# Attention heads: strict turns between VectorE and GpSimd, a 672/352 split, and one row maximum a step over 1024 columns

## The reference, cut to what matters

```python
qn = _scramble(qn); kn = _scramble(kn)                       # 64 rows a head
helical = jnp.einsum('bhpsc,bhptc->bhst', qn, kn) / p
dot = jnp.einsum('bshd,bthd->bhst', qh, kh) / math.sqrt(hd)
attn = jax.nn.softmax(0.5 * dot + 0.5 * helical, axis=-1)
out = jnp.einsum('bhst,bthd->bshd', attn, vh).reshape(b, s, e)
return out @ Wo.T + bo
```

## Time and profile before

| what | us |
|---|---|
| median of 3 runs (5178.03 to 5193.08) | 5188.1 |
| the profiled execution's own time | 5184.21 |
| its span, first to last instruction | 5182.4 |
| first `probs` to last `high` of the attention heads | 2652.7 to 4842.8 |
| VectorE busy over the span | 4091.0 (79%) |
| TensorE busy (matmuls) over the span | 3695.5 (71%) |
| ScalarE busy | 3058.9 (59%) |
| GpSimd busy | 2570.1 (50%) |

### The profile page before, as it was taken

The page is one execution under the profiler, slowest core; times in us unless marked ns, Lnnn a source line. Parts: engine busy times, 40 slices in busy tenths (PEclk is TensorE's granted clock), DMA queues, the critical chain, the costliest instruction groups (busy, mean ns, idle before and its releaser), DMA issues. The chain is left out here.

```text
span 5182.4 us, 68093 instructions
## 1 busy us (share of the span) xinstructions
PE 3695.5 (71%) x15374; PEld 1420.1 (27%) x15374; DVE 4091.0 (79%) x7784; ACT 3058.9 (59%) x4256; POOL 2570.1 (50%) x2075
## 2 busy tenths in 40 slices
PE   7984002222322697897679999999999999999568
PEld 3431001211212242343223333333333333333123
DVE  5535969999998455358789999999999999998352
ACT  5566212222221454245649898989989898999342
POOL 1000757777777101204626666666666666666312
PEclk9997556666666898999979999999999999999779
DMA  1015653333432200012431111111111111100300
GB/s 45 6 45 118 114 117 75 86 79 75 91 75 56 72 13 10 0 72 102 163 62 36 36 35 36 36 29 27 36 36 36 36 35 36 36 21 5 106 10 33
DMA packets 126542, 276.41 MB, mean 53 GB/s; under 512 B 41296, under 2 KB 70864, under 8 KB 117904
## 3 DMA queue, kind: packets, MB, share of 16 engines
q1 hardware_dynamic: 124208, 263.05, 21.4%
q10 hardware_dynamic: 1952, 9.18, 0.6%
HBM read 178.65 MB, written 93.36 MB: 52 GB/s over the span
## 5 line engine op out<-in xcount | busy, mean ns | idle before, releaser
L1027 POOL TENSOR_TENSOR att_heads_rest<-att_heads_probs,att_heads_high 128x576 f16<-128x576 f32 x1024 | 1393.1, 1361 | 830.9 <-ACT att_heads_high L1114 824.3
L1144 DVE TENSOR_REDUCE att_heads_maxima<-att_heads_peek 128x1 f32<-128x512 f32 x2048 | 1311.2, 680 | 94.2 <-PE att_heads_peek L1040 66.6
L1112 ACT ACTIVATE att_heads_probs<-att_heads_scores 128x1024 f32<-128x1024 f32 x1024 | 1073.4, 1048 | 242.3 <-PE att_heads_scores L1058 233.9
L1058 PE MATMUL att_heads_scores<-att_heads_q,att_heads_k 128*128 128x512 f16 (+1 forms) x4096 | 1065.4, 382 | 32.4 <-issue 20.6
L1114 ACT ACTIVATE att_heads_high<-att_heads_scores 128x1024 f16<-128x1024 f32 x1024 | 1074.5, 1049 | 0.0
L1164 DVE TENSOR_TENSOR att_heads_rest<-att_heads_probs,att_heads_high 128x448 f16<-128x448 f32 x1024 | 897.2, 877 | 58.2 <-POOL att_heads_rest L1027 43.8
L1843 PE MATMUL delta_scan_sums<-delta_scan_o_halves,main_identity 128*128 128x256 f32 x768 | 243.8, 491 | 956.1 <-POOL delta_scan_o_halves L1918 956.1
L1040 PE MATMUL att_heads_peek<-att_heads_k,att_heads_q 112*128 112x512 f16 x2048 | 684.2, 395 | 90.1 <-DVE att_heads_maxima L1144 48.3
L1058 PEld LDWEIGHTS att_heads_scores<-att_heads_q,att_heads_k 128*128 128x128 f16 (+1 forms) x4096 | 394.4, 98 | 455.7 <-ACT att_heads_high L1114 38.4
L1843 PEld LDWEIGHTS delta_scan_sums<-delta_scan_o_halves,main_identity 128*128 128x128 f32 x768 | 193.3, 257 | 1007.2 <-POOL delta_scan_o_halves L1918 969.4
L1074 PE MATMUL att_heads_out<-att_heads_high,att_heads_v_head 128*64 128x512 f16 x2048 | 418.2, 405 | 5.2 <-DVE att_heads_rest L1164 4.3
(11 more groups left out here) (245 smaller groups left out, 5043.1 us busy)
## 6 DMA issues: line engine op xcount, KB each, us to landing
delta_scan_record<-delta_record SPq DMA_DIRECT2D x64, 1026.0 KB, 10.9
att_heads_q<-att_hel SPq DMA_DIRECT2D x192, 128.0 KB, 3.1
att_heads_k<-att_hel SPq DMA_DIRECT2D x192, 128.0 KB, 3.3
delta_record<-delta_chunks_record SPq DMA_DIRECT2D x64, 256.5 KB, 4.8
att_hel<-att_hel_high SPq DMA_DIRECT2D x32, 512.0 KB, 4.4
att_hel<-att_hel_rest SPq DMA_DIRECT2D x32, 512.0 KB, 5.0
att_o<-att_heads_out_copy SPq DMA_DIRECT2D x256, 32.0 KB
att_out_parts<-att_o ACTq DMA_DIRECT2D x8, 1024.0 KB, 13.4
```

What stands on the lines that cost most here:

```text
L1027: nc.gpsimd.tensor_tensor(rest[:, step % 4, SPLIT:], probs[:, step % 4, SPLIT:], high[:, step % 4, SPLIT:], ALU.subtract).then_inc(rest_b_ ...
L1058: mm = nc.tensor.matmul(scores[:, step % 2, tokens(j)], k[0:rows, slot, number, tile * P:(tile + 1) * P], q[0:rows, slot, number, tokens(h ...
L1112: nc.scalar.activation(probs[:, step % 4], scores[:, step % 2], ACT.Exp, scale=LOGIT_SCALE).then_inc(probs_ready, 1)
L1144: nc.vector.tensor_reduce(maxima[:, m:m + 1], peek[:, m % 2], AX.X, ALU.max).then_inc(peek_read, 1)
```

## The change: what it does

VectorE takes 672 columns of `rest` and GpSimd 352. GpSimd's part of a step now also waits until VectorE has done its part of the step before. A peek goes over 1024 keys: two matmuls into the two banks, then one reduce over both; there is one in each step, 32 in a head, with a credit of 1, so that TensorE writes the pair when the reduce before has ended. The last peek of a head is in step 22; the shift is turned in step 24, as before, and the shift row is made in step 24, behind the reduce. ScalarE copies a half's output five steps after its last score instead of two. The first 32 peeks of head 0 take turns in three buffers, the peek's and the two of the scores. The loads of the first three heads each wait for one more memset instead of all four. `EARLY` becomes 9.

```diff
--- before.py
+++ after.py
@@ -910,7 +910,7 @@
         high = s.sb("high", [P, 4, T // 2], F16)
         rest = s.sb("rest", [P, 4, T // 2], F16)
         v_head = s.sb("v_head", [P, SLOTS, QT, WIDE], F16)
-        maxima = s.sb("maxima", [P, QT * 4])
+        maxima = s.sb("maxima", [P, QT * 2])
         tile_max = s.sb("tile_max", [P, QT])
         shift_row = s.sb("shift_row", [QT, P], F16)
         out_copy = s.sb("out_copy", [P, 2, BLK])
@@ -929,22 +929,25 @@
         STEPS = 2 * QT
         QUADS = BH // SLOTS
         AHEAD = 3
-        BEFORE_COPY = 2
-        PEEKS = QT * 4
-        LAST_PEEKS = 23
-        EARLY = PEEKS - 2 * (LAST_PEEKS + 1)
-        TURN_AT = LAST_PEEKS + 1
-        ROWS_AT = TURN_AT + 1
+        BEFORE_COPY = 5
+        PEEKS = QT * 2
+        LAST_PEEKS = 22
+        EARLY = PEEKS - (LAST_PEEKS + 1)
+        TURN_AT = LAST_PEEKS + 2
         LOADS = 18 * 16
-        SPLIT = 448
-
-        W_CREDIT, H_CREDIT, R_CREDIT, K_CREDIT, O_CREDIT = 2 * STEPS, 4, 4, 2, 2
+        SPLIT = 672
+
+        W_CREDIT, H_CREDIT, R_CREDIT, K_CREDIT, O_CREDIT = 2 * STEPS, 4, 4, 1, 2
 
         def peeks_at(step):
 
             if step <= LAST_PEEKS:
-                return 1, range(EARLY + 2 * step, EARLY + 2 * step + 2)
-            return 2, range(2 * (step - TURN_AT), 2 * (step - TURN_AT) + 2)
+                return 1, range(EARLY + step, EARLY + step + 1)
+            return 2, range(step - LAST_PEEKS - 1, step - LAST_PEEKS)
+
+        def first_bank(m):
+
+            return (peek[:].rearrange("p j n -> p (j n)"), scores[:, 0], scores[:, 1])[m % 3]
 
         def later(quad, slot, by):
 
@@ -1000,9 +1003,10 @@
                         store_shift(*later(quad, slot, 1))
                     store_out(quad, slot, 1)
 
+                for slot in range(3):
+                    sp.wait_ge(ones_ready, slot + 1)
+                    load(0, slot)
                 sp.wait_ge(ones_ready, SLOTS)
-                for slot in range(3):
-                    load(0, slot)
                 store_shift(0, 0)
                 with sp.Fori(0, QUADS - 1) as quad:
                     for slot in range(SLOTS):
@@ -1024,21 +1028,37 @@
                         nc.gpsimd.tensor_copy(v_head[:, slot, :, 0:V_COLS], v[:, bass.ds(head, 1)].squeeze(1)).then_inc(v_ready, 1)
                         for step in range(STEPS):
                             pool.wait_ge(high_ready, head * STEPS + step + 1 + H_CREDIT)
+                            pool.wait_ge(rest_a_ready, head * STEPS + step + R_CREDIT)
                             nc.gpsimd.tensor_tensor(rest[:, step % 4, SPLIT:], probs[:, step % 4, SPLIT:], high[:, step % 4, SPLIT:],
                                                     ALU.subtract).then_inc(rest_b_ready, 1)
 
             @block.tensor
             def _(pe):
+                def first_peeks():
+
+                    pe.wait_ge(loaded[0], LOADS)
+                    for m in range(PEEKS):
+                        tile, part = divmod(m, 2)
+                        bank = first_bank(m)
+                        if m >= 3:
+                            pe.wait_ge(peek_read, m - 2 + K_CREDIT)
+                        for j in range(2):
+                            mm = nc.tensor.matmul(bank[:, tokens(j)], q[0:MAX_ROW, 0, 0, tile * P:(tile + 1) * P], k[0:MAX_ROW, 0, 0, tokens(part * 2 + j)],
+                                                  start=True, stop=True)
+                        mm.then_inc(peek_ready, 1)
+
                 def peek_scores(quad, slot, numbers):
 
                     head = quad * SLOTS + slot
                     for m in numbers:
-                        tile, blk = divmod(m, 4)
+                        tile, part = divmod(m, 2)
                         if m == 0:
                             pe.wait_ge(loaded[slot], (quad + 1) * LOADS)
                         pe.wait_ge(peek_read, head * PEEKS + m + 1)
-                        nc.tensor.matmul(peek[:, m % 2], q[0:MAX_ROW, slot, 0, tile * P:(tile + 1) * P], k[0:MAX_ROW, slot, 0, tokens(blk)],
-                                         start=True, stop=True).then_inc(peek_ready, 1)
+                        for j in range(2):
+                            mm = nc.tensor.matmul(peek[:, j], q[0:MAX_ROW, slot, 0, tile * P:(tile + 1) * P], k[0:MAX_ROW, slot, 0, tokens(part * 2 + j)],
+                                                  start=True, stop=True)
+                        mm.then_inc(peek_ready, 1)
 
                 def turn_shifts(quad, slot):
 
@@ -1089,7 +1109,7 @@
                         peek_scores(*later(quad, slot, by), peeks)
 
                 pe.sem_inc(weighed, W_CREDIT)
-                peek_scores(0, 0, range(PEEKS))
+                first_peeks()
                 turn_shifts(0, 0)
                 for step in range(AHEAD):
                     score(0, 0, step)
@@ -1141,12 +1161,12 @@
                         dve.wait_ge(peek_ready, head * PEEKS + m + 1)
                         if m == 0:
                             dve.wait_ge(max_step, head + 1)
-                        nc.vector.tensor_reduce(maxima[:, m:m + 1], peek[:, m % 2], AX.X, ALU.max).then_inc(peek_read, 1)
+                        nc.vector.tensor_reduce(maxima[:, m:m + 1], peek[:].rearrange("p j n -> p (j n)"), AX.X, ALU.max).then_inc(peek_read, 1)
 
                 def shifts(quad, slot):
                     head = quad * SLOTS + slot
                     dve.wait_ge(peek_read, (head + 1) * PEEKS + K_CREDIT)
-                    nc.vector.tensor_reduce(tile_max[:], maxima[:].rearrange("p (t b) -> p t b", b=4), AX.X, ALU.max).then_inc(max_step, 1)
+                    nc.vector.tensor_reduce(tile_max[:], maxima[:].rearrange("p (t b) -> p t b", b=2), AX.X, ALU.max).then_inc(max_step, 1)
 
                 def shift_rows(quad, slot, first=False):
                     head = quad * SLOTS + slot
@@ -1170,10 +1190,10 @@
                         if exists(last, slot, 1) or step + 1 < STEPS:
                             split(head, step + 1)
                         by, numbers = peeks_at(step)
-                        if step == ROWS_AT and exists(last, slot, 1):
-                            shift_rows(*later(quad, slot, 1))
                         if exists(last, slot, by):
                             read_peeks(*later(quad, slot, by), numbers)
+                        if step == TURN_AT and exists(last, slot, 1):
+                            shift_rows(*later(quad, slot, 1))
                         if step == LAST_PEEKS and exists(last, slot, 1):
                             shifts(*later(quad, slot, 1))
 
@@ -1184,7 +1204,11 @@
                 dve.sem_inc(rest_a_ready, R_CREDIT)
                 for half in range(2):
                     dve.sem_inc(out_stored[half], 1)
-                read_peeks(0, 0, range(PEEKS))
+                for m in range(PEEKS):
+                    dve.wait_ge(peek_ready, m + 1)
+                    if m == 0:
+                        dve.wait_ge(max_step, 1)
+                    nc.vector.tensor_reduce(maxima[:, m:m + 1], first_bank(m), AX.X, ALU.max).then_inc(peek_read, 1)
                 shifts(0, 0)
                 shift_rows(0, 0, True)
                 read_peeks(0, 1, range(EARLY))
```

## The result

The changed kernel takes 5055.4 us (median of 4 runs, 5052.8 to 5065.6) against 5190.6 before (4 runs): ratio 0.9747, 95% interval 0.9725 to 0.9769. The profiled execution took 5052.8, 131 less than the 5184.2 of the one before.

The account below looks back on a forecast made before the run. TensorE was taken as the floor at 1.956 us a step; 3.95 less a head over 31 heads (122) plus 5.5 at the start, 128 from 5184.2, gave 5056, with the median 3.9 above: 5060 us, range 5035 to 5135.

Parts of the forecast that it names:

- The bound: Attention heads: TensorE is the floor at 1.956 us a step, with VectorE, turns and peek cycles of 1.91, 1.87, 1.92 under it.
- What a head lost before: Old heads, 67.2 against 62.6 us: 4.6 lost to the turned shift, waits before output copies, and 2.3 of collisions.
- The turns' cycle: VectorE's and GpSimd's parts of `rest` in strict turns: 0.85 each plus hand-overs 0.07 and 0.10, 1.87 us, slack 0.08.
- A head: One attention head: 62.6 + 0.27 (turn) + 0.13 (shift row) + 0.26 (copy of values) = 63.25 us, against 67.2 before.
- The late copy: ScalarE's output copies five steps late: waits of 1.03 go, and with them 0.54 us a head on TensorE.
- The turn's place: Turn of the shift in TensorE's step 24, last reduce in VectorE's step 22: 1.49 us of idle time goes.
- The start: Ahead of the steps: loads 6.4 us less, first peeks 8.1 less, early peeks of head 1 9 more; together -5.5.
- (A): Rival, chance 0.17: one of the tight cycles sets the pace, a step of 2.03, 74 us more, 5134.
- (B): Rival, chance 0.05: no change, since VectorE's operations don't overlap; cycle 2.09, head 67.3, time about 5183 us.
- (D): Rival, chance 0.08: more is won, small delays hide in each other, 62.6 us a head, 5037.
- (E): Rival, chance counted in the forecast: collisions stay elsewhere, as a split against the copy of the values, once a head.
- (C): Rival, chance 0.06: slower, the turns bound; nothing gained at 2.08 a step, 5403 us if GpSimd's part stays at 1.28.

Follow-up runs that it names:

- e10: Changed kernel with the values copied by DMA on SyncE's queue instead of by GpSimd: 5063.2 us, ratio 0.9765.
- e12: Changed kernel with values by DMA, early peeks ahead of the first scores, last head without turns, GpSimd's loop over single heads: 5039.8 us, ratio 0.9723.
- e4: Changed kernel with ScalarE's copy of a half's output back at two steps after its last score instead of five: 5064.2 us, ratio 0.9763.
- e8: Changed kernel with the shift turned in step 23 instead of 24, shift row still in step 24: 5084.0 us, ratio 0.9800.
- e5: Changed kernel with peeks and start as before, two reduces of 512 a step; turns, 672 columns and late copies kept: 5072.4 us, ratio 0.9777.
- e6: Changed kernel with VectorE's part at 640 columns and GpSimd's at 384: 5081.9 us, ratio 0.9803.
- e7: Changed kernel with VectorE's part at 736 columns and GpSimd's at 288: 5065.5 us, ratio 0.9767.
- e2: Kernel before the change (448/576 columns) with only GpSimd's wait on VectorE's part of the step before added: 5256.8 us, ratio 1.0127.
- e3: Changed kernel with VectorE's part back at 448 columns and GpSimd's at 576, turns kept: 5232.3 us, ratio 1.0082.
- e1: Changed kernel with GpSimd's wait on VectorE's part of the step before taken out, nothing else: 5176.4 us, ratio 0.9978.

## Why the prediction was right, step by step

- **The bound.** TensorE at 1.956 a step was the floor and is now the pace; all three prices of the step came out within 0.01: split 0.86 (0.85), GpSimd's part 0.85 (0.85), reduce 1.22 (1.22). Collisions are gone, but for the one with the copy of the values, in 24 heads.
- **What a head lost before.** The prediction put 2.3 down to collisions without a row that stood for it. The score starts of the kernel before, in a head of 67.2, bear it out: five steps are 0.45 longer than 1.956, which is 2.3; the turn's step is 1.76 longer; 0.25 and 0.28 at two more steps are the size that was put on the two copies.
- **The turns' cycle** was the term that was mis-sized: 1.87 by the sum, 1.96 measured. The hand-over from VectorE to GpSimd is 0.15, not 0.07: in the last head the split ends at 4691.71 and GpSimd starts at 4691.86. I had read 0.07 off ScalarE to GpSimd. So the slack I gave as 0.08 is none. It cost nothing in heads with peeks, as 1.96 is TensorE's step too. It costs the last head, where the kernel before went at ScalarE's 1.83: 5 us from the last turn to the last copy (73.2 before, 78.4 after), where I had put nothing. TensorE does wait there, ahead of the weigh:

```profile
4691.77 0.41 PE L1094 MATMUL att_heads_out<-att_heads_high,att_heads_v_head 128*64 128x512 f16 x2 [0.36 <-DVE att_heads_rest L1184]
```

- **A head**: 63.25 forecast, 63.2 to 63.55 measured. Copy of the values 0.33 for 0.26, turn 0.16 for 0.27, shift row 0.12 for 0.13. Not forecast: 0.25 and 0.3 in two of four slots, at the same step in every quad. VectorE's timeline in the one with 0.3:

```profile
2801.10 1.23 DVE L1164 TENSOR_REDUCE att_heads_maxima<-att_heads_peek 128x1 f32<-128x1024 f32 x1
2802.61 0.86 DVE L1184 TENSOR_TENSOR att_heads_rest<-att_heads_probs,att_heads_high 128x672 f16<-128x672 f32 x1 [0.29 <-issue]
```

  VectorE waits for nothing that the profile shows. In the slot with 0.25 it is GpSimd that comes late, 0.43 after the split's end instead of 0.15, and VectorE waits for it:

```profile
3006.01 0.85 POOL L1032 TENSOR_TENSOR att_heads_rest<-att_heads_probs,att_heads_high 128x352 f16<-128x352 f32 x1 [1.40 <-DVE att_heads_rest L1184]
...
3006.96 0.86 DVE L1184 TENSOR_TENSOR att_heads_rest<-att_heads_probs,att_heads_high 128x672 f16<-128x672 f32 x1 [0.25 <-POOL att_heads_rest L1032]
```

  The second goes with GpSimd's code: in e10, where GpSimd has one instruction less in each head, it comes two steps later, and in e12, where GpSimd's loop is over single heads, it is gone, while VectorE's own stays. That it is the code's loading is a guess, not shown.
- **The late copy** was counted with 0.54 a head, 0.27 for each half; e4 shows 0.27 for one half alone.
- **The turn's place**: the idle time went, as forecast; e8 gives the worth of the step between the last reduce and the turn.
- **The start**: from first memset to first turn 66.6 before and 52.2 after, 14.4 less for 14.5 forecast; from there to the first weigh 9.7 more for 9.
- **A quad's start** I left as it was. It adds about 5.4 now and 6.1 before, 0.7 less, six times.
- **The sum.** In the attention heads: -14.4 until the first turn, 2127.1 to 2012.5 from first to last turn, +5.2 behind it: 123.8 less, for the 128 forecast. The two profiled executions differ by 131 and the medians by 135. The rest lies in stages that the change doesn't touch (the part behind the heads took 333.9 before and 324.3 after) and is a difference between executions. The miss of 4.6 us in the median is as small as it is partly by that, which is luck: the stage alone is 4 us short of the forecast, and the rest of the program made up for more than that.
- **The rivals.** (A) fell as a step of 2.03, since 889 of the steps from score to score are 1.96; but the margins were as thin as it said, and e5, e6 and e7 each have another cycle as the pace at 1.97 to 1.99. (B) fell: the reduce starts at 2799.14, the split of 0.86 started at 2798.35, 0.07 of overlap. The rule of a drain in the Trainium skill, "VectorE: DVE Perf Modes", Terms, taken as no start before the end of the record ahead, doesn't agree with these two rows. (Its price was summed 3 us low: 0.1 more in each of 31 heads, less 5.5 at the start, is 5186, not 5183.) (D) fell: the small delays don't hide in each other, they are 0.61 a head for the 0.66 forecast. (E) was in the sum, and its collision with the copy is there. (C) was the nearest: its decision point of 2.08 lies between 672 columns (1.96) and 448 (2.15), and e2 and e3, both slower than before, show that it is real where the split is the old one.

## What to carry to other kernels

A VectorE operation with two inputs in SBUF whose mean is well over its shortest, with GpSimd at work beside it, is waiting inside the instruction: put GpSimd's part under an operation that reads PSUM. A wait that orders two engines is itself a cycle (both durations and both hand-overs), and it pays only if that sum is under the step of whoever bounds the kernel: the same line of code was worth 2.3% in the kernel with 672 columns and cost 1.3% in the kernel before, with 448. When several cycles tie, the losses from undoing the parts one by one (121, 177 and 29 us for turns, split and the turn's place) add up to far more than the whole gain of 135, and small delays that had been free (a copy, a small reduce) each appear in the time.

## What the runs showed of the hardware

- Once VectorE's split meets a running GpSimd operation of two inputs, or GpSimd's copy of float16, it does nearly all its work after that one's end: 0.48 of 0.61, 0.72 of 0.86 in e1, 0.71 of 0.86 behind the copy. In the changed kernel the reduces from PSUM beside GpSimd took 1.20 to 1.23, and those with GpSimd idle 1.22 to 1.23. The waiting is reported as busy time of the split.
- Hand-over from VectorE to GpSimd 0.15, from GpSimd to VectorE 0.10. Both durations and 0.25 give every cycle measured within 0.01: 0.61 + 1.28 (2.15), 0.83 + 0.91 (1.99), 0.86 + 0.85 (1.96), 0.92 + 0.73 (1.91).
- GpSimd's part of `rest` (a float32 and a float16 tile into float16) took 0.73 for 288 columns (e7), 0.85 for 352, 0.91 for 384 (e6), 1.28 for 576, and the like operation on 1024 columns in the stage before took 2.13: 0.18 and 1.9 ns a column, as the prediction had it from the last two.
